# Two-layer transformer block in fp32 on one core: x1's sums and one lower half on GpSimd, output banks swapped, h's first turn inside ff2

## The reference

```
y0 = layernorm(x)                                        # no gain
y1 = layernorm(y0 + attention(y0, y0, y0, causal)) * g1 + beta1
y2 = layernorm(y1 + attention(y1, ctx, ctx)) * g2 + beta2
h  = relu(y2 @ w1 + b1)                                  # 256 -> 1024
y3 = layernorm(y2 + h @ w2 + b2) * g3 + beta3
x1 = x + y3
xn = layernorm(x1)
g, u = fp4(xn) @ fp4(w_gate).T, fp4(xn) @ fp4(w_up).T    # 256 -> 704
x2 = x1 + fp4(silu(g) * u) @ fp4(w_down).T               # 704 -> 256
```

## Time and profile before

| | |
|---|---|
| three runs | 652.23, 654.45, 656.27 us (median 654.45) |
| profiled execution | 657.65 us, span 655.8 us |
| TensorE matmul busy | 598.2 us (91%), 3829 instructions |
| VectorE busy | 491.7 us (75%), 1234 |
| ACT busy | 379.8 us (58%), 781 |
| GpSimd busy | 345.3 us (53%), 416 |
| DMA | 19.28 MB, 29 GB/s |
| mean granted TensorE clock | 0.968 of 2.4 GHz |

### The profile page before, as it was taken

One profiled execution on the slowest core, in us unless ns is written; L12 is line 12 of the kernel. 1 busy time (PEld: TensorE's weight loads), 2 busy tenths in 40 slices (PEclk: granted clock), 3 DMA queues, 4 the chain that ended last, 5 costly groups with the idle time before them and its releaser, 6 DMA issues.

```text
span 655.8 us, 11970 instructions
## 1 busy us (share of the span) xinstructions
PE 598.2 (91%) x3829; PEld 541.6 (83%) x3829; DVE 491.7 (75%) x1234; ACT 379.8 (58%) x781; POOL 345.3 (53%) x416
## 2 busy tenths in 40 slices
PE   4876779999999999999999999999999999989766
PEld 3765769898989898898989898988989898979564
DVE  3688668687778878787869777787878777877652
ACT  3456365566738575666657474766557673746331
POOL 2555364465546555575547555655646554654522
PEclk9977899999999999999999999999999999999977
DMA  7601001010100002010101010010100010000000
GB/s 231 198 1 32 1 7 35 1 49 1 43 16 26 25 1 56 0 48 0 56 0 37 11 32 24 0 48 0 56 2 33 1 33 1 10 8 9 9 16 16
DMA packets 18741, 19.28 MB, mean 29 GB/s; under 512 B 1536, under 2 KB 18192, under 8 KB 18704
## 3 DMA queue, kind: packets, MB, share of 16 engines
q1 hardware_dynamic: 18704, 18.82, 9.5%
HBM read 14.62 MB, written 4.19 MB: 29 GB/s over the span
## 4 chain that ended last, share of the span: by engine, by line
PE 70%; DVE 13%; issue 7%; ACT 5%; POOL 2%; DMA 1%; SPq 1%; DVEq 0%; ACTq 0%; POOLq 0%
PE O L1007 13%; PE O L962 6%; PE R L981 5%; PE TR L802 4%; PE R L983 4%; PE R L982 4%; PE R L802 4%; PE R L914 4%; PE R L916 4%; PE R L915 4%; PE O L1027 3%; PE O L1025 3%; PE O L1026 3%; DVE hT_lo L1327 3%; PE R L941 2%
## 5 line engine op out<-in xcount | busy, mean ns | idle before, releaser
L1007 PE MATMUL O<-wd_all,hqT 128*128 128x256 f32 (+1 forms) x384 | 97.5, 397 | 3.3 <-ACT hqT L668 2.7
L451 POOL TENSOR_TENSOR rs<-mv,neg_half 128x1 f32<-128x1 f32 (+1 forms) x112 | 69.5, 626 | 52.9 <-DVE mv L1247 51.4
L914 PE MATMUL R<-gu_hi,xqT_hi 128*128 128x352 f32 x256 | 87.4, 341 | 3.6 <-issue 2.7
L1007 PEld LDWEIGHTS O<-wd_all,hqT 128*128 128x128 f32 (+1 forms) x384 | 70.2, 193 | 23.2 <-issue 11.7
L981 PE MATMUL R<-y2T_hi,w_hi 128*128 128x256 f32 x256 | 78.5, 307 | 7.0 <-DVE y2T_lo L1375 5.0
L916 PE MATMUL R<-gu_hi,xqT_lo 128*128 128x352 f32 x256 | 84.0, 328 | 0.0
L915 PE MATMUL R<-gu_lo,xqT_hi 128*128 128x352 f32 x256 | 83.9, 328 | 0.0
L457 POOL TENSOR_TENSOR hs<-hh,h_rec 128x704 f32<-128x704 f32 x32 | 44.6, 1393 | 74.7 <-DVE h_rec L1283 74.7
L668 ACT ACTIVATE hqT<-R 128x768 f32<-128x768 f32 x32 | 26.0, 813 | 99.2 <-PE R L802 99.2
L1025 PE MATMUL O<-w_hi,hT_hi 128*128 128x256 f32 x256 | 73.9, 289 | 0.0
L983 PE MATMUL R<-y2T_hi,w_lo 128*128 128x256 f32 x256 | 72.7, 284 | 0.0
(11 more groups left out here) (140 smaller groups left out, 1596.7 us busy)
## 6 DMA issues: line engine op xcount, KB each, us to landing
x_in<-in_x SPq DMA_DIRECT2D x16, 256.0 KB, 2.8
x_res<-in_x SPq DMA_DIRECT2D x16, 256.0 KB, 2.8
out<-x SPq DMA_DIRECT2D x32, 128.0 KB, 1.7
ctx_rows<-in_ctx SPq DMA_DIRECT2D x16, 64.0 KB, 2.5
hT<-in_L_xattn_w SPq DMA_DIRECT2D x1, 1024.0 KB, 8.2
hh<-in_L_xattn_w SPq DMA_DIRECT2D x1, 768.0 KB, 7.6
wd_raw<-in_L_ffn_w_down SPq DMA_DIRECT2D x1, 704.0 KB, 9.2
w_raw<-in_L_ffn_w_gate SPq DMA_DIRECT2D x1, 640.0 KB, 4.5
```

What stands on the lines that cost most here:

```text
L451: pool.tensor_tensor(rs[i][:, t0:t0 + len(ts)], mv[i][:, t0:t0 + len(ts), 1], neg_half[:, 0:len(ts)], ALU.pow).then_inc(ln_rstd[i], 1)
L914: mm(o, xh, gu_hi[:, c, m, cols], start=(c == 0), stop=False)
L1007: last = mm(o, hqT[0:w, t, P * i:P * (i + 1)], wd_all[0:w, i, :], start=(i == 0), stop=(i == IC - 1))
```

## The change

Six edits, all in the order of work and in who does it; the arithmetic is the same.

1. Both `x1_sum` of a unit go from VectorE to GpSimd, each right behind its `gamma3`. They wait in addition for the x2 of an earlier unit, and `ff_sum` for the x1 sum of the unit before.
2. The lower half of the last two of h's eight chunks (j = 3) goes from VectorE to GpSimd, behind `scale_h` of t = 0; it has a semaphore of its own.
3. `values` and `down` of row tile t write O[t] instead of O[1 - t], and the waits for the banks' last readers are swapped with them.
4. ff2 of t = 1 is cut after two of its eight f: the first two stand ahead of the first turn of h and of the context's turn, the rest behind.
5. On ACT `norm_x` goes behind the copy of the turned n2.
6. VectorE's order: `z3_stats(1)`, `self_reciprocal(1)` and `self_sum(1)` earlier, `down_add(1)` behind the first `xT_lower`, `cross_max` ahead of `h_lift(0)`, `h_max(1)`, `h_scale(1)` and `h_reciprocal(1)` between `cp_lower` and `ff_sum(0)`, `shift(2)` ahead of `ff_sum(1)`.

```diff
@@ -222,7 +222,8 @@
 
         z2_set, y2_set = sem("z2_set"), sem("y2_set")
         n2_turned, y2T_hi_set, y2T_lo_set = sem("n2_turned"), sem("y2T_hi_set"), sem("y2T_lo_set")
-        ff1_done, relu_set, h_hi_set, h_lo_set = sem("ff1_done"), sem("relu_set"), sem("h_hi_set"), sem("h_lo_set")
+        ff1_done, relu_set, h_hi_set, h_lo_set, h_lo_last = (sem(n) for n in (
+            "ff1_done", "relu_set", "h_hi_set", "h_lo_set", "h_lo_last"))
         ff2_done, z3_set = sem("ff2_done"), sem("z3_set")
         xb_set, y3_set, x1_set = sem("xb_set"), sem("y3_set"), sem("x1_set")
         xq_amax, xq_div, xq_rec = sem("xq_amax"), sem("xq_div"), sem("xq_rec")
@@ -242,6 +243,7 @@
 
         A, F, Q = 1, 2, 3
         FF2_CUT = 5 * FC // 8
+        FF2_TURN = FC // 4
         FIRST = 3
         DIAG, FULL = 2, 3
         TURNED = 2 * 512
@@ -481,6 +483,11 @@
                 pool.affine_select(out=v, in_=v, compare_op=ALU.is_ge, fill=0.0, base=0,
                                    pattern=[[0, 2], [1, P]], channel_multiplier=-1).then_inc(masked, 1)
 
+            def h_lower_last(b, h):
+                wait(pool, h_hi_set, b, h, F, 4, 4)
+                pool.tensor_tensor(hT_lo[:, 6:8, :], hT[:, 6:8, :], hT_hi[:, 6:8, :].bitcast(F32),
+                                   ALU.subtract).then_inc(h_lo_last, 1)
+
             def residual(b, h):
 
                 pool.wait_ge(xres_in[h], b * 16)
@@ -502,6 +509,7 @@
                 prepare(b, h, "early")
                 if f1:
                     gamma3(b, g, 0)
+                    x1_sum(b, g, 0)
                 if q1:
                     unscale_h(b, g, 1)
                 if f1:
@@ -509,6 +517,7 @@
                     power(3, b, g, F, (1,))
                     scale_x(b, g, 0)
                     gamma3(b, g, 1)
+                    x1_sum(b, g, 1)
                     unscale_x(b, g, 0)
                     power(4, b, g, F, (1,))
                 if f:
@@ -534,6 +543,8 @@
                 prepare(b, h, "mid")
                 if q:
                     scale_h(b, h, 0)
+                if f:
+                    h_lower_last(b, h)
                 if a:
                     if isinstance(b, int) and HALVES * b + h == A:
                         pool.wait_ge(g1_in, 16)
@@ -555,6 +566,13 @@
             def gamma3(b, h, t):
                 wait(pool, ln_out[3], b, h, F, T, t + 1)
                 pool.tensor_tensor(z3[:, t, :], z3[:, t, :], g3_row[:], ALU.mult).then_inc(y3_set, 1)
+
+            def x1_sum(b, h, t):
+
+                wait(pool, y3_set, b, h, F, T, t + 1)
+                wait(pool, xb_set, b, h, F, T, t + 1)
+                wait(pool, x2_set, b, h, Q + 1, T, t + 1)
+                pool.tensor_tensor(x1[(h - F) % 2][:, t, :], z3[:, t, :], xb[:, t, :], ALU.add).then_inc(x1_set, 1)
 
             def scale_x(b, h, t):
                 wait(pool, xq_rec, b, h, F, T, t + 1)
@@ -722,14 +740,14 @@
                 prepare(b, h, "early")
                 if f1:
                     norm(3, b, g, F, 0, T, z3[:, 0, :], z3[:, 0, :])
-                if front:
-                    norm_x(b, h)
                 if f:
                     if isinstance(b, int) and HALVES * b + h == F:
                         act.wait_ge(b1_fold_set, 1)
                     wait(act, n2_turned, b, h, F, 1, 1)
                     act.activation(y2T_hi[:], TR[1][:].rearrange("p (c r) -> p c r", c=KC),
                                    ACT.Copy).then_inc(y2T_hi_set, 1)
+                if front:
+                    norm_x(b, h)
                 if q1:
                     copy_hT(b, g, 1)
                 if front:
@@ -949,9 +967,9 @@
                     wait(pe, masked, b, h, A, 1, 1)
                     if half == 1:
                         wait_batch(pe, exp_full, b, 1, 0)
+                    wait(pe, z2_set, b, h, F, T, T)
+                else:
                     wait(pe, z3_set, b, h, F + 1, T, T)
-                else:
-                    wait(pe, z2_set, b, h, F, T, T)
                 lhs = []
                 if half == 1:
                     lhs += [(key, e_full[:, ROWS * key + P * t:ROWS * key + P * (t + 1)]) for key in range(T)]
@@ -959,7 +977,7 @@
                 if t == 1:
                     lhs.append((T * half + 1, e_diag[:, P:2 * P]))
                 for i, (key, e) in enumerate(lhs):
-                    last = mm(O[1 - t][:, 0:D + 1], e, y0[:, key, :], start=(i == 0), stop=(i == len(lhs) - 1))
+                    last = mm(O[t][:, 0:D + 1], e, y0[:, key, :], start=(i == 0), stop=(i == len(lhs) - 1))
                 last.then_inc(pv_done, 1)
 
             def ff1(b, h, js):
@@ -998,10 +1016,10 @@
                 wait(pe, hqT_set, b, h, Q, T, t + 1)
                 wait(pe, z1_set, b, h, A - 1, T, t + 1)
                 if t == 0:
+                    wait(pe, z2_set, b, h, A, T, T)
+                else:
                     wait(pe, z3_set, b, h, F, T, T)
-                else:
-                    wait(pe, z2_set, b, h, A, T, T)
-                o = O[1 - t][:, 0:D]
+                o = O[t][:, 0:D]
                 for i in range(IC):
                     w = min(P, FI - P * i)
                     last = mm(o, hqT[0:w, t, P * i:P * (i + 1)], wd_all[0:w, i, :], start=(i == 0),
@@ -1012,9 +1030,11 @@
                 if t == 0:
                     n = fs[-1] // 2 + 1
                     wait(pe, h_hi_set, b, h, F, 4, n)
-                    wait(pe, h_lo_set, b, h, F, 4, n)
+                    wait(pe, h_lo_set, b, h, F, 3, min(n, 3))
+                    if n == 4:
+                        wait(pe, h_lo_last, b, h, F, 1, 1)
                     if fs[0] == 0:
-                        wait(pe, x2_set, b, h, Q + 1, T, 1)
+                        wait(pe, x2_set, b, h, Q + 1, T, T)
                 else:
                     wait(pe, z3_set, b, h, F, T, 1)
                 o = O[1][:, 0:D]
@@ -1035,7 +1055,7 @@
 
                     wait_batch(pe, ctx_hi_set, b, 1, 1)
                     wait_batch(pe, ctx_lo_set, b, 1, 1)
-                wait(pe, x2_set, b, h, Q + 1, T, T)
+                wait(pe, x2_set, b, h, Q + 1, T, 1)
                 for t in range(T):
                     o = O[0][:, D * t:D * (t + 1)]
                     mm(o, cpT[:, P * t:P * (t + 1)], ctx_hi[:], start=True, stop=False)
@@ -1122,12 +1142,14 @@
                 prepare(b, h, "late")
                 if a:
                     cross_values(b, h)
+                if f:
+                    ff2(b, h, 1, range(FF2_TURN))
                 if q:
                     turn_hq(b, h, 0)
                 if front and h == 0:
                     turn_context(b)
                 if f:
-                    ff2(b, h, 1, range(FC))
+                    ff2(b, h, 1, range(FF2_TURN, FC))
                 prepare(b, h, "end")
 
             slots(pe, slot)
@@ -1331,7 +1353,7 @@
                 wait(dve, down_done, b, h, Q, T, t + 1)
 
                 store_wait(b, h, t)
-                v.tensor_tensor(x2[:, t, :], O[1 - t][:, 0:D], x1[(h - Q) % 2][:, t, :], ALU.add).then_inc(x2_set, 1)
+                v.tensor_tensor(x2[:, t, :], O[t][:, 0:D], x1[(h - Q) % 2][:, t, :], ALU.add).then_inc(x2_set, 1)
 
             def store_wait(b, h, t):
                 wait(dve, x2_out[t], b, h, Q + 1, 16, 16)
@@ -1339,13 +1361,8 @@
             def ff_sum(b, h, t):
                 wait(dve, ff2_done, b, h, F, T, t + 1)
                 wait(dve, y2_set, b, h, F, T, t + 1)
+                wait(dve, x1_set, b, h, F + 1, T, t + 1)
                 v.tensor_tensor(z3[:, t, :], O[1][:, 0:D], y2[t][:], ALU.add).then_inc(z3_set, 1)
-
-            def x1_sum(b, h, t):
-                wait(dve, y3_set, b, h, F, T, t + 1)
-                wait(dve, xb_set, b, h, F, T, t + 1)
-                i = (h - F) % 2
-                v.tensor_tensor(x1[i][:, t, :], z3[:, t, :], xb[:, t, :], ALU.add).then_inc(x1_set, 1)
 
             def x1_stats(b, h, t):
                 wait(dve, x1_set, b, h, F, T, t + 1)
@@ -1377,13 +1394,13 @@
 
             def self_reciprocal(b, h, t):
                 wait(dve, pv_done, b, h, A, T, t + 1)
-                v.reciprocal(rsum1[:, t:t + 1], O[1 - t][:, D:D + 1]).then_inc(rsum1_set, 1)
+                v.reciprocal(rsum1[:, t:t + 1], O[t][:, D:D + 1]).then_inc(rsum1_set, 1)
 
             def self_sum(b, h, t):
 
                 half = 1 - h
                 wait(dve, rsum1_set, b, h, A, T, t + 1)
-                v.scalar_tensor_tensor(z1[:, t, :], O[1 - t][:, 0:D], rsum1[:, t:t + 1],
+                v.scalar_tensor_tensor(z1[:, t, :], O[t][:, 0:D], rsum1[:, t:t + 1],
                                        y0[:, T * half + t, 0:D], ALU.mult, ALU.add).then_inc(z1_set, 1)
 
             def cross_max(b, h):
@@ -1431,24 +1448,23 @@
                     y2T_lower(b, h)
                 prepare(b, h, "ff")
                 if f1:
-                    x1_sum(b, g, 0)
+                    z3_stats(b, g, 1)
                     x1_stats(b, g, 0)
```

(32 more changed lines are left out.)

## The result

The changed kernel takes 661.3 us (median of 5 runs, 659.47 to 661.61), the kernel before beside it 655.3 (5 runs, 652.23 to 656.69): ratio 1.0089 (95% interval in brackets, here and below: [1.0058, 1.0121]), 6.0 us more. The profiled execution took 661.45 (span 659.6), 3.8 more than the one of before.

A forecast was written before the change was run, and what follows sets the result against it. TensorE was taken as the bound, so only its idle time could change. Terms +17.2 - 3.9 - 1.1 - 2.6 - 4.6 - 1.3 + 0.3 = +4.0 us on the median 654.45 gave 658.4 us, range 652.5 to 666.

The forecast's parts named there:

- the likeliest case: The forecast itself, 658.4 us without any rival: range 654 to 663 from wait, ramp and GpSimd bounds, chance 0.66.
- ff2(1) waits behind h_max(1): TensorE's ff2(1) waits for ff_sum(0), queued on VectorE behind h_max(1)'s three steps: 1.32 us in slots 3 to 15, +17.2.
- C: The end of VectorE's cp_lower, said to stay fixed to TensorE; ff2(1) was to start at about C + 2.0.
- The cut priced at nothing: Two f of ff2(1) ahead of h's turn: counted for the wait it uncovers, with no term for the cut itself.
- The turn of ce: cross_max freed on VectorE, so TensorE turns ce earlier: 0.55 in h = 1 (-3.9), 0.15 in h = 0 (-1.1).
- The banks: values(0) starts when ff2 ends, only values(1) waits for ff_sum(1): -2.6 ahead of h = 1 slots, -4.6 ahead of h = 0.
- GpSimd at nothing: GpSimd's added x1 sums and lower half (taken as 1.2 us) stay under cover of 1.4 us or more: 0.
- Ramp: Slot 3: TensorE's 2.84 wait for y2T_lo shrinks by 1.0 as ACT copies n2 first; -1.3 with earlier values.
- `xq(1)` was not late: Rival, slower: down_add(1) ahead of x_lift(1) leaves xq(1)'s product 0.4 before its turn; if late, 663 to 667; chance 0.17.
- The clock: Rival, slower: longer idle ends bring TensorE to 1.2 GHz, 1.3 us a time, 13 times: 675; chance 0.05.
- The covered wait (faster): Rival: ff2(1)'s wait for ff_sum(0) is covered, only gains stay: 641.3, half covered 650; together 0.08.

The follow-up runs named there:

- e1: Changed kernel with ff_sum(0) put back right behind cp_lower, ahead of h_max(1), h_scale(1), h_reciprocal(1): 643.16 us, ratio 0.9794.
- e7: Kernel before with only h_max(1), h_scale(1), h_reciprocal(1) put between cp_lower and ff_sum(0): 665.34 us, ratio 1.0165.
- e3: Changed kernel with ff_sum(0) one step later still, behind cross_sum: 679.54 us, ratio 1.0357.
- e2: Changed kernel with ff2(1) whole again behind h's turn, VectorE's order as changed: 647.63 us, ratio 0.989.
- e6: Changed kernel with ff_sum(0) right behind cp_lower and ff2(1) whole behind h's turn: 638.80 us, ratio 0.975.
- e8: Kernel before with GpSimd's part alone (x1's two sums and the last lower half there): 646.43 us, ratio 0.9883.
- e5: e1 with both x1 sums and the last lower half back on VectorE: 644.85 us, ratio 0.9844.
- e4: Kernel before with only the banks swapped (values, down and their readers use O[t], waits exchanged): 649.08 us, ratio 0.9905.
- e9: e6 with x1's sums and the last lower half back on VectorE as in e5: 643.61 us, ratio 0.9824.
- e10: Changed kernel with ff_sum(0) behind cross_sum and z2's statistics, right ahead of z3_stats(0): 716.08 us in one run.

## Why the prediction was right, and where its sizes were off

The forecast was +4.0, 658.4 us, "within 1%"; measured were +6.0, 661.3, ratio 1.0089, inside the range, and its range of the likeliest case (654 to 663) holds it. The signs that it named came: an idle of 1.36 ended by `ff_sum(0)` once a slot, the turn of `ce` and `values` 0.12 behind their matmuls, the clock at 1.00. That the pair took 73.03 where 73.0 was said is partly luck: the wait and the cut cost about 0.7 a pair more than the prediction's terms, and the turn and the banks won 0.3 more; its own terms add up to 72.85. By steps:

- **ff2(1) waits behind h_max(1): right, undersized.** It starts 2.18 after `cp_lower` ended (403.04 less 400.86), not 2.0. I had subtracted two overlaps of 0.08 between neighbours; here each step starts 0.03 to 0.10 after the end of the one before. From `cross_values` to ff2(1) are 1.65, less the normal 0.12: 1.53 lost a slot instead of 1.32, 13 x 1.53 = +19.9 for +17.2. That it is paid in slots 3 to 15 and taken up by old waits in slots 16 and 17, that C stays fixed to TensorE, and that lighter work on VectorE doesn't shorten it, held. e1, e7 and e3 show this wait to be the cause.
- **The cut priced at nothing: the step that failed.** I counted its order and not itself: 0.13 to 0.17 a slot, about +2. e2 and e6 show it, and the traces of e1 and e6 place it at ff2(1)'s start straight behind `cross_values`, not at the turn inside; why that start takes longer stays open.
- **The turn of ce: right.** 0.61 gained in h = 1 and 0.22 in h = 0, 7 slots each, -5.8 for -5.0. The margins that I left to ACT weren't needed. e8 shows that the lower half on VectorE was what held it up, and e5 that the new place of `cross_max` does the same.
- **The banks: right, a little small.** The head of an h = 0 slot went from 0.80 (0.89 in three of the seven) to 0.12 and its `values` became shorter too, 0.79 to 0.85 together; that of an h = 1 slot lost 0.50 after what t = 1 still waits: 7 x 0.82 + 6 x 0.50 = -8.7 for -7.2. e4 gives the part alone: -6.2 (0.95%).
- **GpSimd at nothing: right for this kernel.** The half took 1.26 to 1.46 (1.2 taken, 0.73 to 1.9 as bounds), x1's sums 0.72 to 0.79 and once 1.26, all under cover; e5 against e1 shows no difference of their medians beyond their spread, and the same pair. Its worth in other company (e8, e9) I hadn't looked for.
- **Ramp: right in kind, its size open.** The wait for `y2T_lo` went from 2.84 to 2.28, so by 0.56 and not by 1.0, as the row of after shows; it is 2.28 or 2.29 in every run with ACT's new order and 2.84 to 2.92 in those without (before, e4, e7, e8). Slot 3 starts 0.96 earlier than before (72.91, 73.87), but it starts at 72.57 in e7 and 72.69 in e8, which lack ACT's edit, so this 0.96 isn't shown to be the change's. ACT's edit was not run alone.

```profile
77.44 0.36 PE L999 MATMUL R<-y2T_hi,w_hi 128*128 128x256 f32 x1 [2.28 <-DVE y2T_lo L1392]
```

Put together, 4.0 + 2.7 (the wait) + 2 (the cut) - 0.8 (the turn) - 1.5 (the banks) + 0.4 (the ramp, by the 0.96; +0.7 by the 0.56) is +6.8, against +6.0 by the medians.

The rivals: `xq(1)` was not late. GpSimd and TensorE of after:

```profile
389.27 0.62 POOL L585 TENSOR_TENSOR xq<-xa,x_div 128x256 f32<-128x256 f32 x1 [3.44 <-DVE xa L1338]
```

```profile
390.38 0.38 PE L820 MATMUL TR<-ident,xq 128*128 128x128 f32 x2
```

It ended 0.49 ahead of its turn, where 0.83 was left before and 0.4 was worked out: no wait. The clock stayed at 1.00 in the pairs with 1.36 of idle, but e3 and e10 show it lowered at 2.14 and above, so the mechanism exists, only not at this idle. The covered wait (faster) did not come; it needed the order of e1. The trace after agrees again with the rule of the Trainium skill, SBUF — State Buffer, section Who interferes with whom, that the prediction draws on: VectorE's `ctx_lo` took 1.29 beside GpSimd's product (395.07 to 396.46) and 0.44 in the trace of before, where that product had ended at 393.15. There it was GpSimd that took longer: its instruction started at 394.25, 0.12 into `ctx_lo`, and took 0.92 us where the same one takes 0.73 after the change. The stretch moved to another instruction; as that one was off TensorE's path, it cost nothing here.

**The best version** is e6: the changed kernel with `ff_sum(0)` right behind `cp_lower` and ff2(1) whole, 638.8 us, 2.5% faster than before and 3.4% faster than the change.

## What to carry to other kernels

Where engines take their work in order, price an edit by the latest instruction that another engine waits for: a 0.42 us reader of a PSUM bank put behind 1.5 us of work that nobody is waiting for cost more than all the other edits won. Put first what frees a bank for the bound engine. Then price cover by cover: moving matmuls away from in front of a consumer uncovers the next sum (e9), and edits that win alone may win nothing together (e8 and e5).

## What the hardware showed that I had not expected

- Six turns of h put inside an ff2 group cost nothing there, but the group's first matmul straight behind `cross_values` instead of behind the turns cost 0.17 us (0.19 and 0.22 between starts instead of 0.12 and 0.12; e1 against e6, pair 70.1 against 69.76), with one idle over 0.1 in the steady part of e1 (0.21) and none in that of e6.
- A single idle per slot of 36 to 41 us was enough to lower the granted clock for a stretch soon behind it, twice in 13 slots at 2.14 us and in every late slot at 3.3 us, at a cost of 1.4 to 2.5 us each time; at 1.36 us it was not.
- The mean granted clock differs from run to run of the same kernel, and the time with it, by up to 8 us: e1 took 638.41 with a mean clock of 0.976 and 646.25 with 0.955, e6 635.87 with 0.976 and 642.1 with 0.963. In the profiled executions of both the steady slots are at 1.00, and the ramp and the tail below: 0.86 up to slot 4 and 0.82 from 570 us on in e1 (the run of 646.25), 0.88 and 0.95 (from 568 us on) in e6 (the run of 638.62). There the same number of matmuls, up to one, was busy in the tail for 61.7 us in e1 and 53.6 in e6.
